# All sixteen mix groups as split float32r products, the halves of e made four groups late, and six re-orderings around them

## The reference

```python
q, k, v = mlp(x, W1q, ...), mlp(x, W1k, ...), mlp(x, W1v, ...)    # h = gelu(x @ W1 + b1); h @ W2 + b2
scores  = tril(q @ k.T / scale)                                   # causal, no softmax
x  = LN(x + LN(scores @ v) * ln_w + ln_b)                         # layer 1: attention; the result is called x1
xn = LN(x) * gamma + beta                                         # layer 2: soft mixture of 16 experts, 16 slots each
logits   = unit(xn) @ unit(mu)                                    # per token 256 numbers, e = exp(logits)
slot_in  = softmax over the tokens(logits).T @ xn                 # over the 2048 tokens of a batch
slot_out = gelu(slot_in @ w1 + b1) @ w2 + b2
out      = LN(x + softmax over the slots(logits) @ slot_out)
```

## Time and profile before

| | |
|---|---|
| median of 3 runs | 585.02 us (585.01 to 585.04) |
| the profiled execution | 584.8 us, of which the span shown is 582.7 |
| busy in the span | PE 565.2 (97%), DVE 489.7 (84%), POOL 421.2 (72%), ACT 406.9 (70%) |
| granted TensorE clock | 0.995 of full speed |
| moved by DMA | 59.64 MB in the span |

### The profile page before, as it was taken

One profiled execution on the slowest core, in us unless ns is written; L12 is line 12 of the kernel. 1 busy time (PEld: TensorE's weight loads), 2 busy tenths in 40 slices (PEclk: granted clock), 3 DMA queues, 4 the chain that ended last, 5 costly groups with the idle time before them and its releaser, 6 DMA issues. The chain is left out here.

```text
span 582.7 us, 12013 instructions
## 1 busy us (share of the span) xinstructions
PE 565.2 (97%) x3892; PEld 525.7 (90%) x3892; DVE 489.7 (84%) x1052; ACT 406.9 (70%) x870; POOL 421.2 (72%) x406
## 2 busy tenths in 40 slices
PE   9999999999999999999999999989999999989992
PEld 7989989999899999999999989979999999978992
DVE  6579889899898889988989889998988777548996
ACT  4765666676767667766667676677679988754884
POOL 0869779798797787977979879785658777453553
PEclk9999999999999999999999999999999999999997
DMA  7424133042240422413304223024776777875965
GB/s 226 92 74 108 20 92 75 36 110 33 76 108 8 100 35 73 108 18 90 74 34 108 31 77 75 9 29 77 153 154 144 145 145 146 141 167 162 323 238 181
DMA packets 166930, 59.64 MB, mean 102 GB/s; under 512 B 139854, under 2 KB 159724, under 8 KB 166892
## 3 DMA queue, kind: packets, MB, share of 16 engines
q1 hardware_dynamic: 166608, 58.89, 43.3%
q10 hardware_dynamic: 284, 0.27, 0.1%
HBM read 27.68 MB, written 14.68 MB: 73 GB/s over the span
## 5 line engine op out<-in xcount | busy, mean ns | idle before, releaser
L529 POOL TENSOR_TENSOR h_lo<-xn_all,h_hi 128x512 fp32r<-128x512 f32 x32 | 41.6, 1301 | 68.0 <-ACT xn_all L645 67.0
L643 ACT ACTIVATE h_hi<-bank,bias_col 128x512 fp32r<-128x512 f32 x96 | 66.5, 692 | 18.7 <-PE bank L800 17.1
L798 PE MATMUL bank<-xnT_hi,w_hi 128*128 128x512 f32 x188 | 76.2, 405 | 0.0
L799 PE MATMUL bank<-xnT_lo,w_hi 128*128 128x512 f32 x188 | 74.4, 396 | 0.0
L800 PE MATMUL bank<-xnT_hi,w_lo 128*128 128x512 f32 x188 | 74.2, 395 | 0.0
L678 ACT CAST state_hi<-bank 128x512 fp32r<-128x512 f32 x57 | 33.6, 589 | 49.1 <-PE bank L933 49.1
L1702 PE MATMUL bank<-xn_all,e_tok 128*128 128x257 f32 x256 | 65.1, 379 | 0.0
L1197 DVE TENSOR_TENSOR state_lo<-bank,state_hi 128x512 fp32r<-128x512 f32 x57 | 39.4, 692 | 29.2 <-ACT state_hi L678 29.2
L1805 DVE STREAM_TRANSPOSE e_turn<-e_tok 128x256 f32<-128x256 f32 x64 | 40.1, 635 | 16.3 <-ACT e_tok L1587 14.8
L1587 ACT ACTIVATE e_tok<-bank,shift,xinv 128x256 f32<-128x256 f32 x64 | 36.2, 566 | 19.1 <-PE bank L1692 12.2
L1702 PEld LDWEIGHTS bank<-xn_all,e_tok 128*128 128x128 f32 x256 | 44.1, 189 | 3.8
(11 more groups left out here) (222 smaller groups left out, 2198.9 us busy)
## 6 DMA issues: line engine op xcount, KB each, us to landing
x_all<-in_L_attn_x SPq DMA_DIRECT2D x16, 512.0 KB, 4.1
kT<-k_turn SPq DMA_DIRECT2D x128, 64.0 KB, 2.5
ET_all<-e_turn SPq DMA_DIRECT2D x64, 128.0 KB, 4.0
xn_all<-in_xT SPq DMA_DIRECT2D x15, 512.0 KB, 4.7
out<-xn_all SPq DMA_DIRECT2D x15, 512.0 KB, 3.8
x_spill<-x_all SPq DMA_DIRECT2D x12, 512.0 KB, 2.9
ET_all<-x_spill SPq DMA_DIRECT2D x8, 512.0 KB, 5.2
w_sb<-in_L_ffn_w SPq DMA_DIRECT2D x2, 512.0 KB, 5.4
```

The lines of the kernel that those rows point to most:

```text
L529: pool.tensor_tensor(h_lo[:, V_SLOT, m, :], hv[:, m, :], h_hi[:, V_SLOT, m, :].bitcast(F32), ALU.subtract).then_inc(hv_split, 1)
L643: nc.scalar.activation(h_hi[:, h_slot(j, n), m, :], ps, ACT.Gelu, bias=bias(n, m))
L798: nc.tensor.matmul(ps, w[0], xs[0], start=start, stop=False, skip_group_check=shared)
L799: nc.tensor.matmul(ps, w[0], xs[1], start=False, stop=False, skip_group_check=shared)
```

## The change

1. **All batches split.** `SPLIT` becomes (0, 1, 2, 3): four more spills, four more reloads, four more casts of `ET_hi`, four more subtractions of `ET_lo`, one more `so_lo`; the 32 plain products of groups 0 to 3 become 96 split ones. x1 is reloaded four groups ahead of its use instead of eight (`AGAIN`). In SP's order a spill now follows the exchange of the same group.
2. **Halves four groups late.** In the route ACT casts and POOL subtracts the halves of the group four before, and not two; five groups are left for the end instead of three, and ACT's casts there are dealt out between the two Gelus and behind them.
3. **Additions turned round.** `add_residual(k)` waits for the shift of k-1.
4. **Table load.** A Gelu of four numbers stands ahead of the last copy of the slots, and so the table is loaded there.
5. **Last slots.** In the last batch each half of the slots is normalised as soon as its own fold is done.
6. **Last attention group.** On DVE, ACT and POOL several steps change places: both v biases go ahead, `sum_v` of the second half moves behind the masking of scores, `floor_norms` goes ahead of `split_xnT`, and POOL makes the last `vsum_lo` before `add_beta`.
7. **Opening.** In group 1, PE's first `chunk` moves behind the next hidden block, and POOL's `split_vsum` ahead of `split_hv`.
8. **First loads.** W1k is issued from ACT's queue and no longer from SP's; DVE clears `zeros` before `v_sum`.

```diff
@@ first loads: SP, ACT, DVE
-                load_weight(WK1, W1k)
+                act.dma_start(w_in[:, WK1, :, :], W1k...).then_inc(weight_loaded[WK1], 16)
+                nc.vector.memset(zeros, 0.0).then_inc(zeros_set, 1)
                 nc.vector.memset(v_sum[:, 0, :], 0.0)
-                nc.vector.memset(zeros, 0.0).then_inc(zeros_set, 1)
@@ POOL, last attention group
+                        split_vsum(a, 1)
                         add_beta(pool, 1, 1)
-                        split_vsum(a, 1)
@@ DVE, last attention group
+                        if not more:
+                            bias_v(g, j, 0)
                         pair_statistics(dve, a, 1)
...
+            sum_v(a, ja, 1)
+            tail_state(2)
             sum_v(a, ja, 2)
-            tail_state(2)
...
+            floor_norms(dve, 0, 0)
             split_xnT(dve, 0, 0)
-            floor_norms(dve, 0, 0)
@@ PE, group 1
-                    if attend:
+                    if opening:
+                        update_state(a, 0, True)
+                    elif attend:
                         chunk(a, ja, ba, 0, p)
                     hidden(g, j, WV1, 0)
+                    if opening:
+                        chunk(a, ja, ba, 0, p, updated=True)
@@ what is split, and the order of spills
-            SPLIT = (1, 2, 3)
+            SPLIT = (0, 1, 2, 3)
-            AGAIN = 2 * GB
+            AGAIN = GB
-            SO_ORDER = (2, 3, 1)
+            SO_ORDER = (0, 2, 3, 1)
                 for g in range(GROUPS):
-                    if g + GB - 1 in SPLIT_GROUPS:
-                        spill_x1(g + GB - 1)
                     exchange_e(g)
+                    spill_x1(g)
@@ the halves: POOL, ACT
-                        if GB * b + q - 2 in SPLIT_GROUPS and not (last and q == GB - 1):
-                            split_e(GB * b + q - 2)
+                        if b > 0 and not (last and q == GB - 1):
+                            split_e(GB * (b - 1) + q)
-                for g in range(GROUPS - GB + 1, GROUPS):
+                for g in range(GROUPS - GB - 1, GROUPS):
                     split_e(g)
-                    if t % GT == GT - 1 and k - 3 in SPLIT_GROUPS and not (last and q == 0):
-                        round_e(k - 3)
+                    if t % GT == GT - 1 and k > GB and not (last and q == 0):
+                        round_e(k - 1 - GB)
-                round_e(GROUPS - GB + 1)
-                round_e(GROUPS - GB + 2)
                 for half in range(2):
+                    for g in ((GROUPS - 5, GROUPS - 4), (GROUPS - 3,))[half]:
+                        round_e(g)
...
+                round_e(GROUPS - 2)
                 round_e(GROUPS - 1)
@@ POOL, mix
                     pool.wait_ge(mix_scaled, k + 1)
+                    if k > 0:
+                        pool.wait_ge(y_shift, k)
@@ ACT and DVE, end of the route
                     if last:
+                        act.wait_ge(n2_ready, GT * GROUPS + 1)
+                        nc.scalar.activation(square[:, 0, 0:4], square[:, 0, 0:4], ACT.Gelu)
                         copy_slots(b)
...
+                        if b == B - 1 and s == 0:
+                            dve.wait_ge(half_folded, 1)
+                        elif b == B - 1:
+                            dve.wait_ge(tile_folded, TB * b + 2 * TB)
                         nc.vector.reciprocal(colinv[:, s:s + 1], ...).then_inc(colinv_ready, 1)
-                    for s in range(SB):
                         dve.wait_ge(colinv_ready, SB * b + s + 1)
                         nc.vector.tensor_scalar(slot_in[:, s, :], ...)
```

More of the change, by code:

```diff
@@ L587, in body @@
                         invert_o(pool, a, 0)
-                    if attend:
+                    if attend and settle:
                         split_vsum(a, 1)
@@ L601, in body @@
                     split_ktok(g, 0)
-                    if attend:
+                    if attend and more:
                         invert_o(pool, a, 1)
@@ L606, in body @@
                     split_ktok(g, 1)
+                    if not more:
+                        invert_o(pool, a, 1)
                     if more:
@@ L621, in _ @@
                 rows = ((b1k, WK1), (b1q, WQ1), (b1v, WV1))
+                act.dma_start(w_in[:, WK1, :, :], W1k.rearrange("(k p) n -> p k n", p=P)).then_inc(weight_loaded[WK1], 16)
                 for b_row, n in rows:
@@ L726, in body @@
                         round_state(ba, i + 1, tail_hi[1])
+                        round_vsum(a, 0)
                         round_xnT(act, 0, 0)
@@ L778, in body @@
                     if not more:
-                        norms(act, 0, 0, (2, 3))
+                        norms(act, 0, 0, (2,))
                     round_v(g, 0)
+                    if not more:
+                        norms(act, 0, 0, (3,))
                     round_v(g, 1)
-                    if not more:
-                        round_vsum(g, 0)
                     if not attend:
@@ L945, in carry, with chunk @@
                                      skip_group_check=True)
-                def chunk(a, ja, ba, c, p):
+                def chunk(a, ja, ba, c, p, updated=False):
                     i = GT * ja + c
-                    if i == 0:
+                    if i == 0 and not updated:
                         update_state(a, c, True)
@@ L1268, in body @@
                         floor_mu()
-                    bias_v(g, j, 0)
+                    if more:
+                        bias_v(g, j, 0)
+                    else:
+                        bias_v(g, j, 1)
                     if attend:
@@ L1272, in body @@
                         weight_out(a, 3)
+                    if not more:
+                        sum_v(g, j, 0)
+                        return
                     bias_v(g, j, 1)
                     if attend:
-                        if not more:
-                            sum_v(g, j, 0)
-                            sum_v(g, j, 1)
-                            return
                         add_out(dve, a, 2)
@@ L1384, in build @@
             tile_folded = msem("tile_folded")
+            half_folded = msem("half_folded")
             rinv_ready = msem("rinv_ready")
@@ L1455, in spill_x1 @@
                 def spill_x1(g):
-                    sp.wait_ge(tok_scaled, GT * g)
+                    if g >= GB - 1:
+                        sp.wait_ge(tok_scaled, GT * g)
                     n = g - FIRST
@@ L1544, in _ @@
                 pool.wait_ge(e_turned, TILES + GT)
-                pool.wait_ge(e_split, GROUPS - GB - FIRST + 1)
+                pool.wait_ge(e_split, GROUPS - GB - 1)
                 for w in range(2):
@@ L1703, in fold @@
                                                 xn[q][:, t % GT, :], start=(t == 0), stop=(t == TB - 1))
+                        if b == B - 1 and t == TB - 1 and s == 0:
+                            last.then_inc(half_folded, 1)
                     last.then_inc(tile_folded, 1)
@@ L1851, in normalise_slots @@
                 def normalise_slots(b):
-                    dve.wait_ge(tile_folded, TB * b + 2 * TB)
+                    if b < B - 1:
+                        dve.wait_ge(tile_folded, TB * b + 2 * TB)
                     for s in range(SB):
+                        if b == B - 1 and s == 0:
+                            dve.wait_ge(half_folded, 1)
+                        elif b == B - 1:
+                            dve.wait_ge(tile_folded, TB * b + 2 * TB)
                         nc.vector.reciprocal(colinv[:, s:s + 1], fold_ps(b)[s][:, D:D + 1]).then_inc(colinv_ready, 1)
-                    for s in range(SB):
                         dve.wait_ge(colinv_ready, SB * b + s + 1)
```

1 line of the change is left out of this document (removed).

## The result

The change takes **591.19 us** (median of 6 runs, 588.74 to 592.11) where the kernel before takes 585.01 beside it: ratio 1.0107, 95% interval [1.0087, 1.0128]. It is slower by 1.1%; 583.0 was forecast, with a range of 580.2 to 584.8. The profiled execution took 590.76 (span 589.0, mean granted clock 0.988 where it was 0.995).

What follows compares the result with a forecast made beforehand. PE bounds attention and route, a serial engine chain follows, and the slowest of PE, DVE and DMA sets the mix. -0.3 - 0.5 + 0.9 - 0.6 - 1.5 = -2.0 gave a 583.0 us median, range 580.2 to 584.8.

Steps and rivals of the forecast that it cites:

- Opening: Kernel start: W1k on another queue lets x land up to 0.44 earlier; -0.3 us, between 0 and -0.45.
- Last attention group: End of attention: earlier vsum_lo shortens PE's wait of 1.0, but DVE's tail ends the stage; -0.5 us, bounds 0 and -1.5.
- some of the 0.53: Before the route's first logits: part of the 0.53 us between PE being free and their start may go.
- Route: Batch 1, second group: the added subtraction delays the inverse norm and exponentials by 2.2, PE stands; +0.9 us, 0 to 2.2.
- Experts: Slots to outputs: earlier table load and slot normalising bring outputs 0.26 to 0.76 earlier; -0.6 us, bounds 0 and -0.76.
- The last spill: Rival, before the outputs: ACT's last cast waits for group 15's spill, holding so_hi; 586.0 or 588.9 us; chance 0.07.
- 522.1: Between route and mix: latest landing of group 15's spill that costs nothing; later costs one for one.
- the two times worked out there: Group 15's spill landing with one more queued ahead, 525.1 (3.0 late), or two, 528.0 (5.9 late).
- Mix: All sixteen groups: split products at 2.89 plus 0.12 for the addition's wait, 3.01 a period; -1.5 us, from -3.3 to +0.4.
- DMA: Mix: a store and reload take 3.07 at 342 GB/s, four buffers absorb the lag; adds nothing. Rival of DMA bound: 0.17.

Runs made afterwards that it cites:

- E9: The kernel before with parts 4, 5, 7 and 8 alone (table load, last slots, opening, first loads): 581.97 us, ratio 0.9953.
- E1: The change without part 6, the last attention group back in the order of before: 590.48 us, ratio 1.0099 to the kernel before.
- E3: The change with batch 1's second-group subtraction of ET_lo moved behind the next group's addition of beta: 587.47 us, ratio 1.0069 to the kernel before.
- E7: E3 without part 3's wait, so additions of the mix don't wait for the shift: 589.48 us, ratio 1.0111 to the kernel before.
- E8: The kernel before with part 6 alone (the last attention group): 585.89 us, ratio 1.0037.
- E6: E3 with each spill three groups ahead of the exchange, the first three at the route's head: 584.98 us, ratio 1.0025 to the kernel before.
- E13: E9 with one extra clearing on DVE ahead of the sums of group 6: 585.70 us, ratio 1.0032 to the kernel before.
- E12: The change without part 6, with E3's and E6's edits, additions waiting for their group's last sum instead of part 3: 583.57 us, ratio 0.9995 to kernel before.
- E4: The change with group 15's cast moved behind the first scale_mix, its subtraction behind the first inverse deviation: 588.85 us, ratio 1.0084 to the kernel before.

## Why the prediction was wrong

It forecast 2.0 us less and got 6.2 more. By the stretches of the two traces:

| stretch | forecast | measured |
|---|---|---|
| up to the first logits (opening, last attention group) | -0.8 | -0.1 |
| first logits to fourth exponential | 0 | +1.6 |
| fourth to last exponential (rest of the route) | +0.9 | +1.1 |
| last exponential to first sum of the mix (experts) | -0.6 | +2.2 |
| first sum to the end (mix) | -1.5 | +1.5 |

Point by point:

- **Opening (-0.3): right,** a little more. E9's first exponential is 0.48 earlier. Of the twelve traces with these parts, nine have their casts of x 0.30 to 0.56 earlier than before, three (E1, E3, E7) 0.15 or less.
- **Last attention group (-0.5): the step failed.** It took DVE's tail for what sets the start of the route, and as fixed; then it took "some of the 0.53" all the same. Before the change it is PE's end that sets it, and DVE is done 0.36 ahead. Part 6 lets PE end 2 us earlier and DVE's tail end 0.73 later, so that DVE sets the start and the start is 0.37 later (E8 has that part alone, and the same 0.37). Not counted at all: idle time of PE is not free. Behind 2.52 of it the granted clock was half, and the fourth exponential came 1.6 later than it would have. It does so in some runs only: in the profiles of E3, E6, E7 and E8 the same idle time left the clock alone, and what decides it stays open.
- **Route (+0.9): right** at the place that it named. The jump of 2.4 and what was left of it, 1.0, were in its bounds, and E3 removes the jump. Two things it did not have: a wait of PE for `xnT_lo` at the 13th exponential (up to 0.9, in E6), and that a later route makes the last spill later (E3).
- **Experts (-0.6): the term was right and too small** (E9: 1.40 at the first sum less 0.48 that came with the opening, 0.92, over its bound of 0.76). In the change it was buried.
- **The last spill: the rival that I gave 0.07 came true.** Place and mechanism were as written: casts in order, exchange and spill of group 15, waited for beyond 522.1. The spill landed at 526.94, between the two times worked out there, 4.8 late; one for one that alone would give 587.8. What its argument against it overlooked is SP's own time. I took landing times of 2.9 and 4.0, which are medians over the whole kernel, and nothing for the issue, though the spill was moved behind four exchanges of four issues each and the loads of the second weights; there an exchange of four issues alone took 5.17 and 7.82, and the trace before already had one issue of 3.46. E6 puts the spills ahead: 1.0069 to 1.0025, and the stretch is back at 15.93. And behind this wait, 3.42 for PE, the clock fell again and the first group took 4.99; that is no longer one for one.
- **Mix (-1.5): the step failed twice,** though the gain that it was after is there: groups 1 to 3 take 9.29 and not 10.35. The wait was priced at 0.12, the time from the addition's old start to the shift's end. It costs 0.24: POOL starts 0.13 after the shift's end (559.83 against 559.54 + 0.16), and that was left out. And 2.89 was taken for the pace of split products; it is the mean of six periods of 2.84 to 2.88 and one of 3.12. E13 shows that 2.85 is one of two gaits. In the early one the addition is released by ACT's scaling, which waits for PE's products (551.15 + 0.48, the addition at 551.70 in E9), and the shift is there first (551.64). Once DVE has fallen behind by less than a microsecond, the addition is waiting when POOL ends the inverse deviation, goes first, holds the shift for 0.63, and with 3.21 DVE stays behind. In the kernel before, the 0.22 for a store at 560.66 stands where the late gait begins; so it was the trigger, as E13 makes likely, not a store as such (in E8 it begins without one). In an all-split mix DVE is behind from the first group (E7).
- **DMA: right that it adds nothing at this pace.** E12 issues a pair of 1.049 MB every 3.00 us, with the queues full; the windows show 344 GB/s, the stores of the steady groups land 3.9 to 5.4 behind their issue, and only the last group waits for one, 0.48. In E1 two sums near the end waited, 0.17 and 0.66. So the 342 GB/s of the earlier trace rows is neither refuted nor confirmed as a ceiling: four buffers take up a small lag, as was written. The Trainium skill, "DMA: Bandwidth & Descriptors", section "Where 436 GB/s comes from", has a limit of about 358 there, against which I had preferred the row; this measurement does not contradict it.

The largest error was to see the stretch between route and mix as a chain of engines and to leave out its queue: 2.8 from the last exponential to the first sum, and 1.5 more in the mix's first group.

## What to carry to other kernels

A transfer put on a queue costs its issue time too, and where the queue is backed up that can be several times the usual one: look at the queue's own line in the stretch where it will stand, and keep what an engine with an in-order program waits for ahead of bulky transfers, not behind. Look which engine ends a stage last before shortening one: ending TensorE's work earlier while another engine's tail moves later only lengthens an idle gap, and the clock may charge for it. A period that differs between stretches of the same code may be a gait: find out what order turns it, and compare the price of a wait that fixes the order (0.15 to 0.24 a group here) with what it prevents (0.36). And when an experiment moves a step, look what the moved step delays at its new place: E4's did.

The best version here is E9: the small parts alone on the kernel before, 0.9953 [0.9937, 0.9970].

## What the runs showed that was not expected

- One delay of 0.91 on DVE cost 3.25 by group 14 (E13).
- The same idle time of PE, 2.5 us at the same instant, was followed by a granted clock of 0.50 in the change and in E4, and by 1.00 in the profiled runs of E3, E6, E7 and E8.
- One issue of an exchange on SP's queue took 4.62 us, nearly six times the median; behind the same two loads it took 3.46 in the kernel before.
- A shift of 128x4 on DVE took 2.35 behind the start of a subtraction of 2.39 on POOL (E4), 0.63 behind that of an addition of 0.64 (E7), and 0.16 where it came first.
